# Row maxima of two attention units found during the projection ahead of them, and paced gathers and loads

## The chip, the cores and the metric

The kernel runs on one core of a Trainium2 chip. The metric is the time of one execution on the device in microseconds (us). The engines are TensorE (PE, matrix products and transposes), VectorE (DVE), ScalarE (ACT), GpSimd (POOL) and SyncE (SP, which only issues transfers here). They run side by side and wait for one another by semaphores.

## The reference

Two layers, cut to what is computed. `x` is 2 x 2048 tokens of 256 values.

```python
x  = L0_attn_x
xn = layernorm(x)
s  = linear_attention(xn, W_qkv, W_out)       # elu features, 16 heads
g  = silu(block(xn, ...))                     # 4 x 512 softmax heads of 16, then 8 experts:
                                              #   x + moe(layernorm(x + attn @ Wproj))
x  = x + s * g
xn = layernorm(x)
q, k, v = ((xn @ W).reshape(B, N, 16, 32).transpose(0, 2, 1, 3) for W in (Wq, Wk, Wv))
scores = where(causal, q @ k.T / sqrt(16), -inf)          # 2 x 16 heads, 2048 x 2048
s  = (softmax(scores) @ v) ... @ Wo
w  = simulate_quantize_int4(kernel)
g  = silu(xn @ w + bias + (xn @ a) @ b)
return x + s * g
```

## The kernel before

The program is a sequence of stages, each with one instruction stream for each engine, written out in the order in which that engine works: the first projection, an attention with heads of 16 values, a projection and gate, the routing, the experts (1171 to 1632 us of the trace), `combine_and_project` (1636 to 1899), `wide_attention` (1902.7 to 2947) and the output. The change touches the last four of them but the output.

*Marks.* In `combine_and_project` every engine has a list of names (`pe_names`, `act_names`, `dve_names`). `step(name, ...)` raises that engine's semaphore; `pe_s.wait(act, "s 4")` makes ACT wait until PE has done everything up to `s 4`. A name is a job and a number: `nT m` turns two tiles of the first attention's result (pair m, 16 of them), `s m` is the product of that pair with `w_out`; then for each block b of 512 tokens (8 of them) `qA`, `qB`, `kA`, `kB`, `vA`, `vB` are the halves of the three projections, `T b+1` turns the normalised block for the next round, `y b` is the feed-forward product. Jobs take PSUM banks in turn from two pools: `bank` (3 of them) for the products and `rot` (a single one) for the turnings. A job can take a bank only when the engine named beside the job before has emptied it.

*Combining stage* (the first part of it). PE alternates `nT` and `s`. ACT copies both out of PSUM (L2562, L2567). POOL gathers the experts' rows for 32 tiles, two indirect transfers each (L2549), into four places of two halves; the first eight wait for `nT n+1`. SP loads x (L2507) and the weights, each behind a mark of PE. DVE forms `mixed` (gates by gathered rows, L2640 and L2642), `x` (L2657, L2659), the moments, and `z`, the normalised block (L2678).

*Projection*. For each block ACT takes the upper half (`hi`, f16) of q and k out of the bank, DVE the rest (`lo`, L2685); so q and k are stored as two f16 parts each, `qhi`, `qlo`, `khi`, `klo` (L2532). Blocks 0 to 3 are batch 0, 4 to 7 batch 1. When block 4 comes to be stored, SP loads all that the attention's first group needs (six parts of q and k, four small rows, V; `load_group`) into the tiles `carried.q`, `carried.k` and `carried.v`.

*Second attention* (`wide_attention`). The 32 heads are 8 groups of four; each group has four units, unit u being the 512 queries from 512u on. A unit goes through these steps: score items `S` (PE at L1032, into one of three banks `at_s`), of which DVE takes the row maxima: at L966 where the causal mask is added (the last key block of a unit), at L972 where it is not; a sum of maxima and a shift `M`; the turning `T` of the shifts on PE (L1068), copied by DVE into a strip (L995) that SP writes into two more rows of q with four transfers (L862); then key tiles `ST` (PE, L1040 and the mask at L1044), whose result ACT turns into exponentials (L946), and products with V (L1094). The eviction of a unit is at L928. Which of these comes next on PE is set by a planner in `wide_schedule`, which simulates the engines with assumed costs and writes one list, `body`, that all engines follow. `T` of a unit can only come when all its maxima are known, and `ST` only when its strip has been written.

*Loads of the attention*. SP issues all seven loads of a group at one place: group 1 behind the second strip, group g+2 when group g has ended.

## Time and profile before

| | |
|---|---|
| three runs | 2997.93, 3001.39, 3002.08 us; median 3001.39 |
| the profiled execution | 3008.54 us, its span in the trace 3006.4 us |
| mean granted clock of PE | 0.969 |
| PE busy | 2831.9 us (94% of the span), 18017 matmuls |
| DVE busy | 2010.2 us (67%) |
| ACT busy | 1545.3 us (51%) |
| POOL busy | 990.0 us (33%) |
| DMA | 200.77 MB, mean 67 GB/s |
| chain that ended last, points of the span by engine | PE 29, DVE 4, ACT 1, issue 1, POOL 1 |

### The profile page before, as it was taken

The numbers are of one execution on the slowest core, as the hardware profiler recorded it, in microseconds if no ns is written. First come the engines' busy times: TensorE is split into PE (matmuls) and PEld (weight loads), VectorE is DVE, ScalarE is ACT, GpSimd is POOL, SyncE is SP. The second block draws the span as 40 slices with busy tenths as digits, with TensorE's granted clock in tenths as the row PEclk, the third lists the DMA queues.
The fourth block names the chain that finished last, engine by engine and source line by source line (L and its number), as shares of the span: only waits on it lengthen the run. The fifth ranks groups of instructions, "written<-read, shape, count | busy, mean of one in ns | idle before, by whom it ended". The sixth has DMA issues, their size and how long they took to land. (4 is left out here: it accounts for less than half of the span.)

```text
span 3006.4 us, 46248 instructions
## 1 busy us (share of the span) xinstructions
PE 2831.9 (94%) x18017; PEld 1317.3 (44%) x18017; DVE 2010.2 (67%) x4329; ACT 1545.3 (51%) x2581; POOL 990.0 (33%) x533
## 2 busy tenths in 40 slices
PE   7998999999999976999999899899999999999999
PEld 4664233333333344666676545323333333333327
DVE  7887899999999845000000565688787877878823
ACT  3452477676777755222222444345565665565571
POOL 1000000110101103111101330157777777777791
PEclk9997899999999987999999999889999999999999
DMA  4322122133202124232111466312020220202103
GB/s 130 97 77 76 37 51 39 43 62 66 50 24 62 24 68 130 63 86 75 63 48 34 148 193 185 79 32 61 8 64 12 68 64 8 64 12 68 67 12 119
DMA packets 141306, 200.77 MB, mean 67 GB/s; under 512 B 14320, under 2 KB 107904, under 8 KB 138000
## 3 DMA queue, kind: packets, MB, share of 16 engines
q1 hardware_dynamic: 130672, 173.21, 20.9%
q0 software_dynamic: 9056, 24.59, 3.9%
q8 instruction: 143, 2.34, 0.3%
q14 instruction: 75, 0.61, 0.1%
q10 hardware_dynamic: 1360, 0.01, 0.0%
HBM read 121.21 MB, written 76.02 MB: 66 GB/s over the span
## 5 line engine op out<-in xcount | busy, mean ns | idle before, releaser
L946 ACT ACTIVATE at_probs<-at_st 128x512 f32<-128x512 f32 (+3 forms) x1280 | 588.5, 542 | 442.1 <-PE at_st L1040 282.4
L909 POOL TENSOR_TENSOR at_probs<-at_probs 128x2048 f32<-128x2048 f32 (+3 forms) x205 | 725.9, 3546 | 214.7 <-ACT at_probs L946 135.4
L393 DVE TENSOR_REDUCE at_part<-at_s 128x1 f32<-128x512 f32 (+3 forms) x1280 | 690.0, 603 | 63.0 <-PE at_s L431 28.6
L368 ACT ACTIVATE at_probs<-at_st 128x1024 f32<-128x1024 f32 (+3 forms) x640 | 541.6, 895 | 275.4 <-PE at_st L450 141.0
L972 DVE TENSOR_REDUCE at_part<-at_s 128x1 f32<-128x512 f32 x768 | 498.5, 683 | 67.8 <-PE at_s L1032 63.9
L966 DVE CUSTOM_DVE_ANT_0 at_s<-at_s,at_later 128x384 f32<-128x384 f32 (+3 forms) x512 | 246.9, 498 | 103.8 <-PE at_s L1032 102.4
L510 PE MATMUL at_acc<-at_probs,at_v 128*32 128x512 f32 (+3 forms) x2560 | 305.5, 551 | 8.2 <-ACT at_otile L355 7.8
L2358 DVE TENSOR_TENSOR ex_ot<-ex_bank,lin_b 128x512 f32<-128x512 f32 x32 | 22.2, 692 | 426.3 <-PE ex_bank L2388 352.2
L2321 ACT ACTIVATE ex_hT<-ex_bank,ex_b 128x512 f32<-128x512 f32 x128 | 87.9, 687 | 334.7 <-PE ex_bank L2378 332.7
L2378 PE MATMUL ex_bank<-ex_xT,lin_w 128*128 128x512 f32 x512 | 225.5, 598 | 1.0 <-ACT ex_xT L2314 1.0
L2388 PE MATMUL ex_bank<-lin_w,ex_hT 128*128 128x256 f32 x1024 | 223.7, 379 | 0.8 <-ACT ex_hT L2321 0.8
L1032 PE MATMUL at_s<-all_k,all_q 96*128 96x512 f16 (+3 forms) x640 | 199.4, 366 | 15.1 <-DVE at_part L972 6.1
L2388 PEld LDWEIGHTS ex_bank<-lin_w,ex_hT 128*128 128x128 f32 x1024 | 193.9, 190 | 31.1 <-issue 3.8
L1040 PE MATMUL at_st<-all_q,all_k 98*128 98x512 f16 (+3 forms) x640 | 194.9, 362 | 6.6 <-ACT at_probs L946 3.8
L1032 PE MATMUL at_s<-at_kT,at_qT 96*128 96x512 f16 (+3 forms) x640 | 192.3, 356 | 8.3 <-DVE at_part L966 3.8
L431 PE MATMUL at_s<-lin_k_first,lin_q_first 48*128 48x512 f16 (+3 forms) x640 | 184.6, 374 | 14.9 <-DVE at_part L393 5.8
L1040 PE MATMUL at_st<-at_qT,at_kT 98*128 98x512 f16 (+3 forms) x640 | 185.1, 350 | 8.3 <-ACT at_probs L946 6.8
L431 PE MATMUL at_s<-at_kT,at_qT 48*128 48x512 f16 (+3 forms) x640 | 176.4, 361 | 6.9 <-DVE at_part L393 4.2
L1864 POOL DMA_DIRECT2D att_sums<-att x28 | 14.5, 523 | 487.7 <-DMA att<-at_otile 487.7
L2549 POOL DMA_INDIRECT p_rows<-exp_out,all_gather_at x64 | 62.1, 970 | 270.3 <-PE p_rot L2731 182.3
L2378 PEld LDWEIGHTS ex_bank<-ex_xT,lin_w 128*128 128x128 f32 x512 | 98.2, 192 | 118.2 <-issue 117.5
L1094 PE MATMUL at_acc<-at_probs,at_v 128*32 128x512 f32 (+3 forms) x1280 | 144.4, 536 | 4.0 <-ACT at_otile L928 3.8
(342 smaller groups left out, 3950.0 us busy)
## 6 DMA issues: line engine op xcount, KB each, us to landing
att<-at_otile SPq DMA_DIRECT2D x64, 256.0 KB, 2.1
lin_w<-in_W SPq DMA_DIRECT2D x16, 1024.0 KB, 7.5
at_v<-v SPq DMA_DIRECT2D x11, 1024.0 KB, 11.1
v<-pr_vt SPq DMA_DIRECT2D x32, 256.0 KB
exp_out<-ex_ot SPq DMA_DIRECT2D x32, 256.0 KB, 2.1
v<-p_vt SPq DMA_DIRECT2D x32, 256.0 KB, 3.7
p_xs<-in_x SPq DMA_DIRECT2D x8, 512.0 KB, 5.2
qhi<-p_parts SPq DMA_DIRECT2D x8, 512.0 KB
```

Source lines behind the costliest of these rows:

```text
L368: act.activation(probs[:, quad % RING, heads_down * p:heads_down * (p + 1), off:QB], st_ps[n % st_slots][:, :, off:QB], ACT.Exp, scale=EXP ...
L393: dve.tensor_reduce(part[:, w % 2, qt * HG + h, j:j + 1], s_ps[n % S_SLOTS][:, 0:width], AX.X, ALU.max).then_inc(item_free, 1)
L431: mm = pe.matmul(place[:, 0:width], QT[g % 2][rows, h // heads_down, q0:q0 + P], KT[g % 2][rows, h // heads_down, j * QB:j * QB + width], ...
L510: mm = pe.matmul(acc_ps[32 * h:32 * h + 32, off:QB], V[g % 2][:, kc, 32 * h:32 * h + 32], probs[:, quads % RING, h, off:QB], start=kc == 0 ...
L909: pool.tensor_tensor(total, total, probs[:, slots.slot[quad], :, off:QB], ALU.add).then_inc(add_done, 1)
L946: act.activation(probs[:, slots.slot[quad], h, off:QB], st_ps[n % ST_SLOTS][:, off:QB], ACT.Exp, scale=EXP_SCALE).then_inc(exp_done, 1)
L966: dve.tensor_tensor_reduce(out=s_ps[n % S_SLOTS][:, 0:width], in0=s_ps[n % S_SLOTS][:, 0:width], in1=later[:, QB - width:QB], scale=1.0, s ...
L972: dve.tensor_reduce(part[:, w % 2, qt * HG + h, j:j + 1], s_ps[n % S_SLOTS][:, 0:width], AX.X, ALU.max).then_inc(item_free, 1)
L1032: pe.matmul(place[:, 0:width], QT[g % 2][0:K, h, q0:q0 + P], KT[g % 2][0:K, h, j * QB:j * QB + width], start=True, stop=True).then_inc(ite ...
L1040: mm = pe.matmul(place[:, off:QB], KT[g % 2][0:K + 2, h, kc * P:(kc + 1) * P], QT[g % 2][0:K + 2, h, u * QB + off:(u + 1) * QB], start=Tru ...
L2378: mm = pe.matmul(d[:, :], w1[e % 2][:, n, f * P:(f + 1) * P], xT[:, n, cb * QB:(cb + 1) * QB], start=n == 0, stop=n == NF - 1)
L2388: mm = pe.matmul(d[:, t * D:(t + 1) * D], hT[cb][:, n, (2 * m + t) * P:(2 * m + t + 1) * P], w2[e % 2][:, n, :], start=n == 0, stop=n == N ...
```

## The change

Six things are done.

1. The row maxima of group 0's units 0 and 1 (`EARLY = 2`) leave `wide_attention`. They become 20 jobs `S 0` to `S 19` of the projection, each put behind one half of blocks 4 (`y` only), 5, 6 and 7, and each in the single `rot` bank. DVE takes the maxima (`max i`), and the two shifts. PE turns these in that bank (`row 0` behind `vB 5`, `row 1` behind `vB 7`), DVE copies the strips, SP writes them into `carried.q`. `S 0` waits for the six loads of q and k.
2. For that the loads of the first group are split: three parts behind the q stores of block 4, three behind its k stores, the small rows behind its v stores, V behind those of block 5.
3. The gathers of the combining stage wait for PE's marks one after the other, instead of the first eight only and the rest by half sets; SP's loads there come one pair earlier, `silu 0` and `sqrt 0` earlier on ACT, and DVE does the whole of block 0 before block 1's `mixed`.
4. In `wide_attention` the loads of the next group are eight pieces (V in halves), one issued at every fourth `ST`.
5. The planner's assumed delay after a group's last product goes from 12000 to 24000.
6. In the experts, the gathers for the second expert wait for marks of the first.

On PE, blocks 4 to 6 of the projection. L2770 and L2778 are the q, k and v halves, L2749 is `T`, L2788 is `y`; before, from `y 4` to `y 5`:

```order
L2788 MATMUL p_bank<-p_w_ffn,p_xT 128x256 x8
L2770 MATMUL p_bank<-p_xT,p_w 128x512 x16
L2778 MATMUL p_bank<-p_w,p_xT 128x512 x8
L2749 MATMUL p_rot<-all_identf,p_z 128x128 x8
L2788 MATMUL p_bank<-p_w_ffn,p_xT 128x256 x8
```

The same place now, from `y 4` to `kB 5` (L2958 is `y`, L2937 the q and k halves, L2898 an early score job):

```order
L2958 MATMUL p_bank<-p_w_ffn,p_xT 128x256 x8
L2898 MATMUL p_rot<-all_k,all_q 128x128 x4
L2937 MATMUL p_bank<-p_xT,p_w 128x512 x4
L2898 MATMUL p_rot<-all_k,all_q 128x256 x4
L2937 MATMUL p_bank<-p_xT,p_w 128x512 x4
L2898 MATMUL p_rot<-all_k,all_q 128x384 x2
L2937 MATMUL p_bank<-p_xT,p_w 128x512 x4
L2898 MATMUL p_rot<-all_k,all_q 128x384 x2
L2937 MATMUL p_bank<-p_xT,p_w 128x512 x4
L2898 MATMUL p_rot<-all_k,all_q 128x512 x2
```

What was one run of sixteen matmuls is four of four, with a score job in `rot` behind each.

On SP, around block 4, before (L744 are the group's loads of q and k, L2532 the stores):

```order
L744 DMA all_q<-qhi 32x4x2048
L744 DMA all_k<-klo 32x4x2048
L746 DMA all_k<-in_shift_rows 2x2048 x4
L748 DMA all_v<-v 128x2048
L2532 DMA qhi<-p_parts 128x4x512
L2532 DMA qlo<-p_parts 128x4x512
```

and now (L767 the loads, L2617 the stores of q and k, L2624 those of v):

```order
L2617 DMA qhi<-p_parts 128x4x512
L2617 DMA qlo<-p_parts 128x4x512
L767 DMA all_q<-qhi 32x4x2048
L767 DMA all_k<-khi 32x4x2048
L767 DMA all_q<-qlo 32x4x2048
L2617 DMA khi<-p_parts 128x4x512
L2617 DMA klo<-p_parts 128x4x512
L767 DMA all_k<-khi 32x4x2048
L767 DMA all_q<-qhi 32x4x2048
L767 DMA all_k<-klo 32x4x2048
L2624 DMA v<-p_vt 128x4x128 x4
```

All loads stood ahead of block 4's stores; they now stand three behind the q stores and three behind the k stores, in the same queue.

On PE, at the start of the second attention, before (L1032 `S`, L1068 `T`; the masked items of unit 0 first, by width):

```order
L1032 MATMUL at_s<-all_k,all_q 128x128 x4
L1032 MATMUL at_s<-all_k,all_q 128x256 x4
L1032 MATMUL at_s<-all_k,all_q 128x384 x4
L1032 MATMUL at_s<-all_k,all_q 128x512 x5
L1032 MATMUL at_s<-all_k,all_q 128x128
L1032 MATMUL at_s<-all_k,all_q 128x512
L1032 MATMUL at_s<-all_k,all_q 128x128
L1068 MATMUL at_s<-all_ident_f,at_shift 8x128 x4
```

and now (L1074 `S`, L1082 and L1086 `ST` and its mask):

```order
L1074 MATMUL at_s<-all_k,all_q 128x512 x2
L1074 MATMUL at_s<-all_k,all_q 128x128
L1082 MATMUL at_st<-all_q,all_k 128x512
L1086 MATMUL at_st<-all_mask_kq,all_ident 128x128
L1082 MATMUL at_st<-all_q,all_k 128x512
L1086 MATMUL at_st<-all_mask_kq,all_ident 128x128
```

Key tiles of unit 0 now come after three items (of unit 2) instead of twenty and a turning. By count, the items and key tiles that stand ahead of each `T` are: before, unit (0,0) 20 and 0, (0,1) 52 and 16, (0,2) 100 and 48, (0,3) 164 and 96, (1,2) 212 and 132; now (0,2) 52 and 48, (0,3) 116 and 96, (1,2) 164 and 160, (1,3) 244 and 224. From (2,1) on, 389 key tiles in, both lists are the same but for the 48 items that left.

The diff, cut to its core:

```diff
@@ -543,6 +543,28 @@
+EARLY = 2
+
+
+def early_jobs_of(u):
+    jobs = []
+    for qt in range(4):
+        for j in range(u + 1):
+            width = QB if j < u else (qt + 1) * P
+            together = 4 if width <= QB // 2 else 2
+            jobs += [(u, qt, h, together, j, width) for h in range(0, HG, together)]
+    return jobs
+
+
+EARLY_JOBS = [job for u in range(EARLY) for job in early_jobs_of(u)]
+EARLY_LAST = [max(i for i, job in enumerate(EARLY_JOBS) if job[0] == u) for u in range(EARLY)]
+EARLY_SLOTS = [(slot, b) for b, slots in ((4, "y"), (5, "qA qB kA kB vA y"), (6, "qA qB kA kB vA vB T y"), (7, "qA qB kA kB vA"))
+               for slot in slots.split()]
+EARLY_AT = {at: i for i, at in enumerate(EARLY_SLOTS)}
+EARLY_TURN = {("vB", 5): 0, ("vB", 7): 1}
+assert len(EARLY_SLOTS) == len(EARLY_JOBS)
+
+
 def wide_schedule():
@@ -638,7 +660,7 @@
                 if g >= 2:
-                    ready = max(ready, pv_end[last_of[g - 2]] + 12000)
+                    ready = max(ready, pv_end[last_of[g - 2]] + 24000)
...
@@ -731,33 +753,40 @@
+    def load_group(self, eng, C, qk, v, n):
         K = 32
...
+        if n < 6:
+            dst, src = (self.q, self.k)[n % 2], (qk[0][0], qk[1][0], qk[0][1], qk[1][0], qk[0][0], qk[1][1])[n]
+            eng.dma_start(dst[n // 2 * K:(n // 2 + 1) * K, :, :], src[0].rearrange("h d t -> d h t")).then_inc(self.qk_ld, 16)
+        elif n == 6:
+            for h in range(HG):
+                eng.dma_start(self.k[3 * K:3 * K + 2, h, :], C["shift_rows"][2 * h:2 * h + 2, h, :]
+                              ).then_inc(self.group_ld, 16)
+        else:
+            eng.dma_start(self.v[:, :, :], v[0, 0]).then_inc(self.group_ld, 16)
...
@@ -827,18 +856,24 @@
-        def load(eng, g):
-            eng.dma_start(V[k][:, :, :], v[g]).then_inc(v_ld[k], 16)
+            if n < 6:
+                r = n // 2
+                dst, src = (QT, KT)[n % 2], (q_hi, k_hi, q_lo, k_hi, q_hi, k_lo)[n]
+                eng.dma_start(dst[k][r * hd:(r + 1) * hd, :, :], src[g].rearrange("h d t -> d h t")).then_inc(qk_ld[k], 16)
+            else:
+                part = slice(NKC // 2 * (n - 6), NKC // 2 * (n - 5))
+                eng.dma_start(V[k][:, part, :], v[g][:, part, :]).then_inc(v_ld[k], 16)
+
+        LOADS, EVERY = 8, 4
...
                             sp.wait_ge(out_stored[k], issued[k])
-                        carried.load_finish(sp, W, out)
+                elif ev[0] == "ST":
+                    pairs += 1
+                    if pairs % EVERY == 0 and group:
+                        if loaded < (LOADS if group < GROUPS else Carried.FINISH_PARTS):
+                            sp.wait_ge(st_ready, pairs)
+                            if group < GROUPS:
+                                load(sp, group, loaded)
+                            else:
+                                carried.load_finish(sp, W, out, loaded)
+                            loaded += 1
+            assert group == GROUPS and loaded == Carried.FINISH_PARTS
             while ended:
...
@@ -2295,8 +2341,10 @@
-            for e, cb in ((0, 1), (1, 0), (1, 1)):
-                gather_tokens(pool, z_rows, rows_at, xin, rows_ld, e, cb)
+            gather_tokens(pool, z_rows, rows_at, xin, rows_ld, 0, 1)
+            for cb, f in ((0, half - 1), (1, NFF - 1)):
+                pe_s.wait(pool, f"h0{f} 0")
+                gather_tokens(pool, z_rows, rows_at, xin, rows_ld, 1, cb)
             for e in range(E - 2):
...
@@ -2413,6 +2461,7 @@
+    GROUP_AT = {(4, "q"): 3, (4, "k"): 3, (4, "v"): 1, (5, "v"): 1}
...
-    act_after = {9: ["silu 0"], 12: ["sqrt 0"], 15: ["silu 1"]}
+    act_after = {7: ["silu 0"], 10: ["sqrt 0"], 15: ["silu 1"]}
...
-    dve_names += ["mixed 0", "x 0", "moments 0", "mixed 1", "z 0", "x 1", "moments 1"]
+    dve_names += ["mixed 0", "x 0", "moments 0", "z 0", "mixed 1", "x 1", "moments 1"]
...
@@ -2506,14 +2591,14 @@
-            pe_s.wait(sp, "s 4")
+            pe_s.wait(sp, "s 3")
             load_x(0)
             for n, name in enumerate(("Wq", "Wk", "Wv")):
-                pe_s.wait(sp, f"s {2 * n + 6}")
+                pe_s.wait(sp, f"s {2 * n + 5}")
                 sp.dma_start(w[:, n], W[name].rearrange("(c p) n -> p c n", p=P)).then_inc(w_ld[0], 16)
             pe_s.wait(sp, "s 11")
             load_x(1)
...
@@ -2524,27 +2609,46 @@
                 for side, name in enumerate("qk"):
                     dve_s.wait(sp, f"lo {name}B {b}")
...
+                    for _ in range(GROUP_AT.get((b, name), 0)):
+                        carried.load_group(sp, C, qk_out, v_out, group)
+                        group += 1
                 act_s.wait(sp, f"vB {b}")
                 for g in range(4):
                     sp.dma_start(v_out[s, g, :, 4 * j:4 * j + 4, :], vt[:, :, g * P:(g + 1) * P]).then_inc(v_kept, 16)
+                for _ in range(GROUP_AT.get((b, "v"), 0)):
+                    carried.load_group(sp, C, qk_out, v_out, group)
+                    group += 1
+                for u in range(EARLY):
+                    if b == NB - EARLY + u:
+                        dve_s.wait(sp, f"strip {u}")
+                        for h in range(HG):
+                            sp.dma_start(carried.q[96:98, h, u * QB:(u + 1) * QB], strip[2 * h:2 * h + 2, u, :]
+                                         ).then_inc(carried.row_ld, 16)
             sp.wait_ge(part_out, 64 * NB)
             sp.wait_ge(v_kept, 64 * NB)
+            sp.wait_ge(carried.row_ld, 16 * HG * EARLY)
 
         @block.gpsimd
...
                 if b >= 2:
                     dve_s.wait(pool, f"mixed {b - 2}")
-                else:
-                    pe_s.wait(pool, f"nT {n + 1}")
+                if 0 < n < 12:
+                    pe_s.wait(pool, f"nT {n + n // 2}" if n < 11 else "T 0")
+                elif n:
+                    pe_s.wait(pool, f"{('qB', 'kB', 'vB', 'y')[t]} {b - 3}")
...
@@ -2632,6 +2736,41 @@
+            def maxima(i):
+                u, qt, h, together, j, width = EARLY_JOBS[i]
+                pe_s.wait(dve, f"S {i}")
+                tile, row = rot.tile(f"S {i}"), qt * HG + h
+                if i == 0:
+                    dve.wait_ge(later_ready, 1)
+                if j < u:
+                    last = dve.tensor_reduce(part[:, u, row:row + 2, j:j + 1], tile[:, :, 0:width], AX.X, ALU.max)
+                else:
+                    for y in range(together):
+                        place = early_place(tile, y, together, width)
+                        last = dve.tensor_tensor_reduce(out=place, in0=place, in1=later[:, QB - width:QB], scale=1.0,
+                                                        scalar=MASK, op0=ALU.add, op1=ALU.max,
+                                                        accum_out=part[:, u, row + y, j:j + 1])
+                step(f"max {i}", last)
+
...
+            def early(s, b):
+                if (s, b) in EARLY_AT:
+                    i = EARLY_AT[s, b]
+                    maxima(i)
+                    if i in EARLY_LAST:
+                        shifts(EARLY_LAST.index(i))
+                if (s, b) in EARLY_TURN:
+                    u = EARLY_TURN[s, b]
+                    pe_s.wait(dve, f"row {u}")
+                    step(f"strip {u}", dve.tensor_copy(strip[:, u, :],
+                                                       rot.tile(f"row {u}")[0:2 * HG, 0, 0:QB // 2].bitcast(F16)))
+
             def mixed_tile(b, t):
...
@@ -2705,13 +2844,19 @@
+                    early("qB", b)
                     lower(0, "q", "B", b)
+                early("kA", b)
                 lower(1, "k", "A", b)
                 if b + 2 < NB:
...
                     combine(b + 2)
                     statistics(b + 2)
+                early("kB", b)
                 lower(1, "k", "B", b)
+                for s in ("vA", "vB", "T"):
+                    early(s, b)
                 pe_s.wait(dve, f"y {b}")
                 if b:
                     act_s.wait(dve, f"g {b - 1}")
...
@@ -2740,6 +2886,27 @@
+
+            def early(s, b):
+                if (s, b) in EARLY_AT:
+                    i = EARLY_AT[s, b]
+                    u, qt, h, together, j, width = EARLY_JOBS[i]
+                    d = rot.take(pe, f"S {i}")
+                    if i == 0:
+                        pe.wait_ge(carried.qk_ld, Carried.QK_LOADS)
+                    for y in range(together):
+                        mm = pe.matmul(early_place(d, y, together, width),
+                                       carried.q[0:96, h + y, u * QB + qt * P:u * QB + (qt + 1) * P],
+                                       carried.k[0:96, h + y, j * QB:j * QB + width], start=True, stop=True)
+                    step(f"S {i}", mm)
+                if (s, b) in EARLY_TURN:
+                    u = EARLY_TURN[s, b]
+                    dve_s.wait(pe, f"shift {u}")
+                    d = rot.take(pe, f"row {u}")[0:2 * HG, 0, 0:QB // 2].bitcast(F16)
+                    for qt in range(4):
+                        mm = pe.transpose(d[:, qt * P:(qt + 1) * P], shift[:, u, qt * HG:(qt + 1) * HG, :]
+                                          .rearrange("p h two -> p (h two)"), C["ident_f16"][:, :])
+                    step(f"row {u}", mm)
 
             def turn(b):
...
```

## Rows read from the trace of the kernel before

**Rows 1.** The timeline of PE in the combining stage (start us, us, engine, instruction, idle before).

```profile
1655.86 0.60 PE L2731 MATMUL p_rot<-all_identf,all_mix 128*128 128x128 f32 x4
1658.02 0.60 PE L2731 MATMUL p_rot<-all_identf,all_mix 128*128 128x128 f32 x4
...
1678.85 0.60 PE L2731 MATMUL p_rot<-all_identf,all_mix 128*128 128x128 f32 x4
```

**Rows 2.** Windows there (PE, PEld, DVE, ACT, POOL busy; granted clock; DMA share; GB/s).

```profile
1660.00:1665.00 5.00, 0.77 (x5) 0.42 (x4) 0.00 (x0) 1.19 (x2) 3.78 (x5) 0.98 0.38 110
1665.00:1670.00 5.00, 3.65 (x11) 2.70 (x9) 0.00 (x0) 0.00 (x0) 3.78 (x5) 0.68 0.40 105
```

**Rows 3.** The timelines of ACT, SP and POOL there, one row each.

```profile
1673.81 0.60 ACT L2567 ACTIVATE all_mix<-p_bank 128x512 f32<-128x512 f32 x1 [9.28 <-remote]
...
1673.80 0.37 SPq L2513 DMA_DIRECT2D p_w<-in_Wk  x1
...
1669.81 0.95 POOL L2549 DMA_INDIRECT p_rows<-exp_out,all_gather_at  x1 [0.30 <-issue]
```

**Rows 4.** The timeline of PE in the projection: starts of blocks 5 and 6.

```profile
1824.05 10.46 PE L2770 MATMUL p_bank<-p_xT,p_w 128*128 128x512 f32 x24
1835.28 3.70 PE L2770 MATMUL p_bank<-p_xT,p_w 128*128 128x512 f32 x8 [0.76 <-DVE p_parts L2685]
...
1850.01 13.90 PE L2770 MATMUL p_bank<-p_xT,p_w 128*128 128x512 f32 x32
```

**Rows 5.** Windows of the second attention, from eviction to eviction.

```profile
1902.70:1942.00 39.30, 31.45 (x142) 10.95 (x143) 33.01 (x106) 8.25 (x18) 7.85 (x5) 0.69 0.04 6
1902.70:2083.10 180.40, 163.10 (x924) 53.84 (x924) 153.51 (x386) 79.75 (x168) 96.06 (x31) 0.86 0.13 30
2209.80:2334.60 124.80, 121.51 (x832) 40.88 (x832) 101.88 (x253) 74.78 (x166) 96.49 (x30) 1.00 0.18 43
```

**Rows 6.** The chain of waits: from the first strip to the first key tile.

```profile
1913.72 0.30 DVE at_strip L995
...
1915.93 1.59 DMA all_q<-at_strip
1917.57 0.61 PE at_st L1040
```

**Rows 7.** The chain of waits: three score matmuls of 512.

```profile
1947.00 0.65 PE at_s L1032 x3
```

**Rows 8.** The chain of waits: row maxima of 128 and of 512 columns.

```profile
1904.37 0.19 DVE at_s L966
...
1910.76 0.59 DVE at_s L966
...
2099.02 1.30 DVE at_part L972 x2
```

**Rows 9.** The timeline of DVE in blocks 5 and 6 of the projection.

```profile
1799.43 0.17 DVE L1195 RECIPROCAL p_rstd<-p_std 128x4 f32<-128x4 f32 x1
...
1805.37 0.48 DVE L2642 SCALAR_TENSOR_TENSOR p_fg<-p_rows,all_gate,p_fg 128x256 f32<-128x256 f32 x1
...
1811.56 1.22 DVE L2657 TENSOR_TENSOR p_fg<-p_fg,all_mix 128x1024 f32<-128x1024 f32 x1
...
1817.02 1.28 DVE L2685 SCALAR_TENSOR_TENSOR p_parts<-p_bank,all_score,p_parts 128x1024 f16<-128x1024 f32 x1
```

**Rows 10.** Windows around the loads of the first group.

```profile
1794.00:1802.00 8.00, 8.00 (x34) 5.43 (x33) 3.54 (x11) 4.24 (x4) 0.00 (x0) 1.00 0.97 297
1802.00:1818.00 16.00, 15.23 (x36) 6.52 (x35) 13.17 (x25) 7.49 (x8) 0.00 (x0) 1.00 1.04 202
```

**Rows 11.** The timeline of SP: block 4's q stores are issued.

```profile
1810.48 0.39 SPq L2532 DMA_DIRECT2D qhi<-p_parts  x1
```

**Rows 12.** The timeline of DVE: the strips of units (0,2) and (0,3).

```profile
1970.02 0.41 DVE L995 COPY at_strip<-at_s 8x512 f16<-8x512 f16 x1
...
2018.56 0.37 DVE L995 COPY at_strip<-at_s 8x512 f16<-8x512 f16 x1
```

More of the change, by code:

```diff
@@ L552, in wide_schedule @@
     ahead, late, count = [], None, {}
-    for unit in units:
+    for unit in units[EARLY:]:
         g, u = unit
@@ L578, in wide_schedule @@
     free, evictions = [0.0, 0.0], []
-    exp_end, pv_end, row_at, add_end, sum_end = [], [], {}, [], []
+    exp_end, pv_end, row_at, add_end, sum_end = [], [], {unit: 0.0 for unit in units[:EARLY]}, [], []
     slots = Slots(units)
@@ L841, in _ @@
             ended, issued = [], [0, 0]
+            pairs, group, loaded = 0, 1, 0
             def store(unit):
@@ L2427, in combine_and_project, with early_turns @@
             jobs.append((f"s {m - 2}", "act", f"s {m - 2}"))
+    turns = [(f"nT {m}", "act", f"nT {m}") for m in range(PAIRS)] + [("T 0", "act", "T 0")]
+    def early_turns(at):
+        if at in EARLY_AT:
+            turns.append((f"S {EARLY_AT[at]}", "dve", f"max {EARLY_AT[at]}"))
+            pe_names.append(turns[-1][0])
+        if at in EARLY_TURN:
+            turns.append((f"row {EARLY_TURN[at]}", "dve", f"strip {EARLY_TURN[at]}"))
+            pe_names.append(turns[-1][0])
     for b in range(NB):
@@ L2496, in combine_and_project @@
         marks = {"act": act_s, "dve": dve_s}
[L2497 to L2498 removed]
+        rot = Banked(c, "rot", [(n, (marks[e], d)) for n, e, d in turns], 1)
         banks = Banked(c, "bank", [(n, (marks[e], d)) for n, e, d in jobs], 3)
@@ L2772, in _ @@
                         step(f"{s}{half} {b}", mm)
+                        early(f"{s}{half}", b)
                 for half in "AB":
```

128 lines of the change are left out of this document (81 added, 47 removed).

## The prediction

> **What bounds the kernel now.** I read the page's shares first, then the windows by stage, then the chain of waits and the timelines at the three places that the change touches. The shares stand in the table above: TensorE (PE) is busy 94% of the span, and of the 36 points that the chain names it has 29. So time is won only where PE stands still, runs at its lower clock, or has less to do. Three places matter.
>
> *Combining stage* (1636 to 1691 us). A turn `nT` and an output projection `s` take 2.17 us together, the distance of the turns at 1655.86 and 1658.02. Then the rhythm breaks: from 1658.02 to the turn at 1678.85 PE does three such pairs in 20.83 us instead of 6.51. 14.3 us are lost [rows 1]. The granted clock reads 0.68 in part of it, so PE worked at the 1.2 GHz level for much of that time, after 5 us in which it was almost idle [rows 2]. ScalarE (ACT), which frees PE's banks here, waited 9.28 us for something that the profile calls only "remote", and SP issued the load of Wk, which waits for PE's mark `s 8`, at 1673.80 although PE had issued that work by 1660.4. PE's marks thus arrived late, while POOL issued gather after gather without a pause, the last at 1669.81 [rows 3].
>
> *Projection* (1691 to 1899 us). PE works at full clock. It has one wait of 0.76 us a block before block 6 and none in blocks 6 and 7 [rows 4]. Whatever is put in here, PE pays at once.
>
> *Start of the second attention.* Up to the eviction of unit (0,0), 39.3 us hold 142 matmuls at a clock of 0.69; up to the eviction of unit (0,3), 180.4 us hold 924. Later a group of four units takes 124.8 us for 832 [rows 5]. At that pace these 924 matmuls would take 138.6 us: 41.8 are lost. The chain shows why. VectorE (DVE) finds the row maxima, PE turns them, SP sends strips, and only 14.9 us after the stage's start does the first key tile run [rows 6].
>
> **Projection, term by term.** The 20 early jobs are 48 matmuls with 18,432 columns in all (5120 for unit 0, 8192 + 5120 for unit 1). Three score matmuls of 512 take 0.65 us [rows 7], so these take 7.8. For the joints between f32 and f16 work I put 0.03 us a job, 0.6, and for the two turns of the shifts 0.3 each. Work: 9.0 us.
>
> The waits come from the single turning bank, which each early job holds until DVE has its maxima. One masked maximum takes DVE 0.25 us for 128 columns (0.19 and the 0.06 that follows it) and 0.65 for 512, two plain ones of 512 take 1.30 [rows 8]. On PE a half block is 3.43 us (32 matmuls in 13.90 with the tail of the last) [rows 4]. Step by step:
> - In block 5 `S 2` comes 7.3 us after `S 0` (two halves and `S 1`). By then DVE has to do four maxima (1.0), z and `mixed 7` (1799.43 to 1805.85, 6.4 [rows 9]) and four maxima of 256 (1.5), and with the hand-over of 0.2 that is 9.1: wait 1.8. The old wait of 0.76 goes in return.
> - `S 5` waits for the maxima of `S 4`, which stand on DVE behind combine and statistics of block 7 (1811.56 to 1817.02, 5.5): 1.9.
> - `T 6` waits for the strip of unit 0: 0.6.
> - In block 6 `T 7` follows `S 12` directly and waits for its maxima, 1.4; `S 13` follows `T 7` and waits for ACT's copy of it, 1.2.
>
> That is 6.9 less 0.8: 6.1 us. The other jobs have a half of 3.43 us between them, more than the 2.6 us of one pair of maxima and one lower half on DVE.
>
> **The load before `S 0`.** `S 0` waits for six loads of 0.52 MB. SP issues three behind the q stores of block 4 and three behind its k stores, in one queue. In the trace these loads run at 202 GB/s with the DMA engines full (share 1.04), stores and what goes with them at 297 [rows 10]. From the q stores at 1810.5 [rows 11]: 1.05 MB of stores 3.5 us, 1.57 MB of loads 7.8, so 1821.8; then k stores 3.5 and k loads 7.8, so 1833.1. PE is ready at about 1824.3, for block 5 starts at 1824.05 now [rows 4]. Wait 8.5 us; DVE stands behind `S 0` too, so hardly any of it is made good. Bounds 0 (the loads are through) and 10. The Trainium skill, "DMA: Bandwidth & Descriptors", section Bandwidth, gives 341 GB/s for a 1 MB transfer; by that estimate the loads would end near 1827, the wait would be 2.3 us and the sum 6 us lower. The trace doesn't agree, with 202 GB/s for the same kind of load.
>
> Projection in all: 9.0 + 6.1 + 8.5 = 23.6 us more; bounds 14 and 27. At its end SP sends unit 1's four strips behind the last v stores. Four issues and a landing of 1.59 take 3.5 us [rows 6], of which I put 0.9 on the path, because ACT's last gate comes beside them; bounds 0 and 3.5.
>
> **Attention.** 48 score items and two turns leave it. Unit (0,2) can be keyed once DVE has its maxima: 48 items and 4 of the next unit, 36 plain ones at 0.65 and 16 masked ones at 0.45 on average, 30.6 us; with the start, the shifts and two units' sums 36 us after the stage's start. Now its strip is copied at 1970.02, 67.3 us after the start: gain 31. From there to unit (0,3)'s strip at 2018.56 the same items stand in both orders: 48.5 us again [rows 12]. After it part is given back. The new order has done every key tile of group 0 before unit (1,2) has its strip, and the same before (1,3). For 3.9 us each time (strip copy at 1913.72 to key tile at 1917.57 [rows 6]) PE has only score items, at DVE's pace. Two such holes: 8 us. From unit (2,1) on both orders are the same. I take 31 - 8 = 23 us; bounds 15 (two more holes) and 50 (the 42 lost, and 8 for the work that leaves).
>
> The attention's loads now go out one for every fourth key tile. Their first use lies some 65 key tiles behind the first load, and SP's strips stand behind at most one load more: 0, bounds -3 and +2.
>
> **Combining stage, priced.** Gathers of two row sets, now issued every 1.25 us (0.95 and the 0.30 before it) [rows 3], follow PE's turns and stop when PE stops. Loads come one pair earlier. If the unbroken run of gathers makes the marks late, the 14.3 us go; I keep 13, because `silu 0` still stands between ACT's turns, only earlier. Bounds -15 and +3: block 3's last gather now waits for `y 0`, its rows land some 4.1 us later (two issues of 1.25 and a landing of 1.59), and DVE comes to them after y, z and six half tiles, 6.6 us (1.22, and 5.4 like 1799.43 to the tile before 1805.37 [rows 9]). If that cover goes, DVE, ACT and `kB` wait. In the experts the second expert's gathers wait for marks of the first one's hidden layer; the eight experts take 461 us, 58 each, so the rows are wanted half an expert or more later, and I count 0.
>
> **Sum.** 23.6 + 0.9 - 23 - 13 = -11.5 us on the profiled execution's 3008.5: 2997.0. The median of the runs shown is 7.1 lower: 2990.
>
> **Rivals.**
> - *Both covers hold (chance 0.22).* The loads are through before `S 0`, and the attention gives nothing back. For: PE comes into the attention at full clock, and only the 4096-byte part of the loads is slow. Against: the full queue at 1802 to 1818, and the order's two holes. 23.6 - 8.5 + 0.9 - 31 - 13 = -28: 2973.
> - *The late marks stay (0.27).* Gathers aren't their cause, or they appear under the profiler alone. For: the DMA engines were 0.40 busy there. Against: they end 3 us after the last gather. 23.6 + 0.9 - 23 = +1.5: 3003.
> - *Bank and load decide, the slower side (0.18).* PE waits for the k loads at `S 0` with DVE behind it, each later job gets the bank late (27 in all), and the holes leave 15 of the start's gain, while half of the combining gain comes: 27 + 0.9 - 15 - 6.5 = +6.4, 3008. It decides from a wait before `S 0` of over 6 us together with a gain at unit (2,1) under 18.
> - The forecast has 0.33.
>
> Likeliest 2990; range 2967 to 3010, the likeliest case's own 2982 to 2999. Less than 0.2% (6 us) can't be told from no change. Faster: all of the first rival, four fifths of the forecast, a tenth of the second, 0.52. Slower: two thirds of the third and a fifth of the second, 0.18. Same: the rest, 0.30.
>
> **What would show it.** Combining: the three pairs in 6.5 us at a clock near 1.0. Before `S 0`: a PE wait of 8 us on a load. Blocks 5 and 6: waits of 1 to 2 us on the turning bank. Attention: first key tile within 2 us, unit (0,2)'s strip 36 us and (0,3)'s 85 us after the start, then 124.8 us a group. I am wrong if the hole stands, if `S 0` doesn't wait, or if the gain at (0,3)'s strip is far from 31 us.

## The result, and the profile after

The changed kernel takes 3007.53 us (median of 20 executions), the kernel before 3001.26 (20, the same chip); ratio 1.0027, interval 1.002 to 1.0034. So it is slower by 6.3 us, where 11.5 less and 2990 were forecast. The profiled execution of the changed kernel took 3011.69, its span is 3010.0.

The two traces, cut at the first turning of the combining stage, at the first matmul of block 0, at the end of `y 7` and at the first score of the second attention (each read from PE's timeline):

| stage, us | before | changed | difference | forecast |
|---|---|---|---|---|
| all ahead of the combining stage | 1636.2 | 1643.7 | +7.5 | 0 |
| combining | 54.6 | 40.5 | -14.1 | -13 |
| projection, blocks 0 to 7 | 208.3 | 241.4 | +33.1 | +23.6 |
| from `y 7` to the first score | 3.9 | 4.5 | +0.6 | +0.9 |
| second attention to its last eviction | 1043.8 | 1020.4 | -23.4 | -23 |
| the rest | 59.6 | 59.6 | 0 | 0 |

The first line shows no effect of the change: in the 18 further profiles below this stretch takes 1635.2 to 1644.3 us, for kernels with and without the change alike. Its last part, from the experts' first matmul on, is where point 6 of the change lies, and it takes 463.8 to 465.4 us in all 20 profiles, so the scatter lies in stages that no edit touches, and point 6 is worth nothing that can be measured. Point 5 was not tried alone. The four lines below the first, in which the change can act, sum to -3.8. So this pair of profiles doesn't hold the result. One thing is odd about the profile of before: its execution, 3008.54 us, is longer than each of the 20 timed ones (2993.6 to 3004.0), and the record doesn't say on which chip it was taken. Something that it shows may be missing from those 20.

*Combining.* Windows of the changed kernel over the stretch that [rows 2] show, and POOL's timeline:

```profile
1660.00:1665.00 5.00, 5.00 (x31) 4.44 (x29) 0.78 (x2) 2.82 (x6) 2.58 (x4) 1.00 0.69 210
```
```profile
1651.95 0.96 POOL L2653 DMA_INDIRECT p_rows<-exp_out,all_gather_at  x1 [2.24 <-PE p_rot L2877]
...
1658.44 0.94 POOL L2653 DMA_INDIRECT p_rows<-exp_out,all_gather_at  x1 [1.79 <-PE p_rot L2877]
```

PE is busy throughout at 1.00, and POOL, which had issued sixteen transfers one behind the other before, now pauses for some 2 us after every four (two sets). The stretch in which PE stands still, called the hole from here on, is gone.

*Projection.* The timeline of PE, blocks 4 to 7:

```profile
1831.79 0.58 PE L2898 MATMUL p_rot<-all_k,all_q 96*128 96x128 f16 x4 [11.88 <-DMA all_k<-klo]
1832.16 5.67 PE L2937 MATMUL p_bank<-p_xT,p_w 128*128 128x512 f32 x8
...
1838.11 3.60 PE L2937 MATMUL p_bank<-p_xT,p_w 128*128 128x512 f32 x8
...
1855.00 0.60 PE L2898 MATMUL p_rot<-all_k,all_q 96*128 96x512 f16 x2 [1.89 <-DVE p_part L2750]
...
1859.95 1.06 PE L2916 MATMUL p_rot<-all_identf,p_z 128*128 128x128 f32 x8 [0.60 <-DVE p_strip L2771]
...
1889.38 1.06 PE L2916 MATMUL p_rot<-all_identf,p_z 128*128 128x128 f32 x8 [1.41 <-DVE p_part L2746]
1891.56 1.04 PE L2898 MATMUL p_rot<-all_k,all_q 96*128 96x512 f16 x2 [1.11 <-ACT p_xT L2686]
1892.39 6.23 PE L2958 MATMUL p_bank<-p_w_ffn,p_xT 128*128 128x256 f32 x16
```

The waits in the bank are where they were forecast and nearly as long (`S 5` 1.89 against 1.9, `T 6` 0.60 against 0.6, `T 7` 1.41 against 1.4, `S 13` 1.11 against 1.2). Two things are not as forecast. `S 0` waited 11.88 us for the last load of k, not 8.5, and after that idle stretch the next eight matmuls took 5.67 instead of 3.60. And `y 6` took 6.23 instead of 3.62 behind the two waits at `T 7` and `S 13`. The windows show the clock there: 0.63 and 0.56 granted in the last two, between the levels of 1.2 and 2.4 GHz.

```profile
1819.00:1832.00 13.00, 1.12 (x8) 0.70 (x7) 1.23 (x1) 1.06 (x1) 1.89 (x2) 0.64 1.06 278
1832.00:1837.70 5.70, 5.70 (x13) 2.46 (x11) 5.01 (x21) 0.00 (x0) 0.00 (x0) 0.63 0.75 202
1892.40:1898.40 6.00, 6.00 (x17) 4.78 (x16) 1.23 (x1) 0.00 (x0) 0.00 (x0) 0.56 0.13 40
```

*Second attention.* The windows that answer to [rows 5], counted from the first score at 1930.0, and the strips of units (0,2) and (0,3), which answer to [rows 12]:

```profile
1930.00:2072.80 142.80, 133.93 (x847) 43.90 (x847) 109.67 (x258) 76.39 (x166) 96.11 (x31) 0.96 0.15 36
...
2212.50:2337.90 125.40, 122.50 (x843) 41.59 (x841) 104.81 (x256) 74.42 (x165) 96.82 (x31) 1.00 0.17 43
```
```profile
1967.80 0.41 DVE L1037 COPY at_strip<-at_s 8x512 f16<-8x512 f16 x1
...
2013.33 0.37 DVE L1037 COPY at_strip<-at_s 8x512 f16<-8x512 f16 x1
```

The first key tile runs 0.9 us after the first score. Unit (0,2)'s strip comes 37.8 us after it (36 were forecast), unit (0,3)'s 83.3 (85 were forecast), 32 less than before. After two groups 24.3 us of that are left, at the end 23.4. The forecast had 31 and 23.

### The profile page after: what moved, and what is told of

Same layout as the page of the kernel before. It is cut to its first block and busy times, and to the rows that moved or that the text cites. A ratio compares the mean times of both kernels' runs of the same rounds, so it can differ in the third digit from the quotient of the medians.

```text
span 3010.0 us, 46280 instructions
## 1 busy us (share of the span) xinstructions
PE 2832.8 (94%) x18017; PEld 1319.8 (44%) x18017; DVE 2014.0 (67%) x4321; ACT 1543.5 (51%) x2581; POOL 988.3 (33%) x535
## 5 line engine op out<-in xcount | busy, mean ns | idle before, releaser
L1014 DVE TENSOR_REDUCE at_part<-at_s 128x1 f32<-128x512 f32 x752 | 487.5, 683 | 67.9 <-PE at_s L1074 63.6
L1008 DVE CUSTOM_DVE_ANT_0 at_s<-at_s,at_later 128x128 f32<-128x128 f32 (+1 forms) x480 | 231.8, 498 | 106.6 <-PE at_s L1074 105.6
L1074 PE MATMUL at_s<-at_kT,at_qT 96*128 96x512 f16 (+3 forms) x640 | 190.6, 354 | 7.7 <-DVE at_part L1014 3.0
L1082 PE MATMUL at_st<-all_q,all_k 98*128 98x512 f16 (+3 forms) x640 | 190.6, 355 | 7.6 <-ACT at_probs L989 4.6
L1082 PE MATMUL at_st<-at_qT,at_kT 98*128 98x512 f16 (+3 forms) x640 | 187.6, 352 | 10.4 <-ACT at_probs L989 7.8
L1074 PE MATMUL at_s<-all_k,all_q 96*128 96x512 f16 (+3 forms) x592 | 178.7, 357 | 10.7 <-PEq L43 4.5
L1140 PE MATMUL at_acc<-at_probs,all_v 128*32 128x512 f32 (+3 forms) x1280 | 143.5, 538 | 2.8 <-ACT at_otile L971 2.8
```

Of the source, the lines that this page charges most:

```text
L1014: dve.tensor_reduce(part[:, w % 2, qt * HG + h, j:j + 1], s_ps[n % S_SLOTS][:, 0:width], AX.X, ALU.max).then_inc(item_free, 1)
L1074: pe.matmul(place[:, 0:width], QT[g % 2][0:K, h, q0:q0 + P], KT[g % 2][0:K, h, j * QB:j * QB + width], start=True, stop=True).then_inc(ite ...
L1082: mm = pe.matmul(place[:, off:QB], KT[g % 2][0:K + 2, h, kc * P:(kc + 1) * P], QT[g % 2][0:K + 2, h, u * QB + off:(u + 1) * QB], start=Tru ...
L1140: mm = pe.matmul(acc_ps[32 * h:32 * h + 32, off:QB], V[g % 2][:, kc, 32 * h:32 * h + 32], probs[:, slots.slot[quads], h, off:QB], start=kc ...
```

## The experiments

Each row gives the median, that of the kernel before in the same call, and the ratio of the two with its interval. Runs without an interval had one execution. The letter says which ran together, and each letter is a chip of its own; the chip of the result above is not on record. a0 and a1 are the changed kernel again, b0 and b1 the kernel before; `_again` and `_third` repeat the run of the same number, and e6 repeats e4, whatever its name says.

| run | us | before | ratio |
|---|---|---|---|
| A e1_combining_only | 3000.29 | 3012.89 | 0.9956 (0.9944 to 0.9969) |
| A e2_without_combining | 3018.29 | 3012.89 | 1.0016 (1.0002 to 1.0030) |
| A e3_loads_first | 2995.05 | 3012.89 | 0.9932 (0.9913 to 0.9950) |
| A e4_attention_loads_at_once | 3006.17 | 3012.89 | 0.9977 (0.9964 to 0.9990) |
| B b0_before_again | 3010.92 | 3014.07 | one execution |
| B a0_after_again | 3005.65 | 3014.07 | 0.9982 (0.9970 to 0.9995) |
| B e5_gathers_only | 2997.76 | 3014.07 | 0.9951 (0.9938 to 0.9963) |
| B e6_loads_first_at_once | 3009.66 | 3014.07 | one execution |
| C a1_after_third | 3007.76 | 3002.49 | 1.0023 (1.0014 to 1.0033) |
| C e3_again | 2997.21 | 3002.49 | 0.9987 (0.9976 to 0.9998) |
| C e7_gathers_only_early | 2998.15 | 3002.49 | 0.9990 (0.9978 to 1.0002) |
| C e8_slot_moved | 2999.97 | 3002.49 | 0.9991 (0.9982 to 1.0000) |
| D b1_before_third | 3009.93 | 3014.84 | one execution |
| D e5_again | 3002.54 | 3014.84 | 0.9954 (0.9937 to 0.9971) |
| D e1_again | 3001.83 | 3014.84 | 0.9954 (0.9937 to 0.9970) |
| D e2_again | 3018.39 | 3014.84 | 1.0011 (0.9999 to 1.0024) |
| E e2_third | 3022.72 | 3014.26 | 1.0019 (1.0005 to 1.0032) |
| E e5_third | 3000.74 | 3014.26 | 0.9957 (0.9945 to 0.9969) |

**e1 and e2, the combining part alone and left out.** e1 is the kernel before with all edits of point 3 of the change and no other; e2 is the changed kernel without them. Of SP's loads in that point four come one pair earlier; the second of x stays, and that of the bias comes one pair later.

> The kernel before with the combining stage's part of the change alone (gathers paced by PE's marks, loads one pair earlier, silu 0 and sqrt 0 earlier, DVE's block 0 whole before block 1). Theory A, the hole of 14.3 us is in every execution of the kernel before and pacing removes it: 14 us faster, ratio about 0.995. Rival B, the hole is in some executions only, or mostly in profiled ones: within 4 us, ratio 0.999 to 1.001. Rival C, pacing costs something that one profile does not show: slower than before.

> The changed kernel with the combining stage's part undone, all else kept. Theory A: 14 us slower than the changed kernel, so 20 to 22 slower than before, ratio 1.007. Rival B: about as the changed kernel, ratio 1.002 to 1.004. Its profile also shows whether the hole comes back in a second program.

e1 is 12.6 us faster than before, e2 5.4 slower. The combining stage takes 41.7 us in e1's profile and 54.9 in e2's. That is theory A for e1. For e2 the forecast of 20 to 22 us slower failed: it is 12.1 us above e4 below, which stands for the changed kernel in this call, but only 5.4 above the kernel before. For here the kernel before takes 3012.89, and it had taken 3001.26.

e2's profile shows one thing more. PE's timeline in e2_again, and POOL's in the changed kernel, of which six transfers fall between block 4's q stores (1806.25) and `S 0` (1831.79):

```profile
1835.95 0.58 PE L2896 MATMUL p_rot<-all_k,all_q 96*128 96x128 f16 x4 [9.32 <-DMA all_k<-klo]
```
```profile
1809.46 1.08 POOL L2653 DMA_INDIRECT p_rows<-exp_out,all_gather_at  x1 [5.85 <-PE p_bank L2937]
...
1821.91 0.94 POOL L2653 DMA_INDIRECT p_rows<-exp_out,all_gather_at  x1 [0.30 <-issue]
```

In e2's three profiles no gather falls there, and `S 0` waits 9.2 to 9.4 us; in the five profiles of the changed kernel and of e4 it waits 11.8 to 12.2. So point 3 costs some 2.5 us of that wait, and the six gathers are what it puts there; that they do it is argued, for e2 undoes the whole point.

**e3, all loads first.** The eight parts of `load_group` go back ahead of block 4's stores:

```diff
+                    for group in range(8):
+                        carried.load_group(sp, C, qk_out, v_out, group)
-                    for _ in range(GROUP_AT.get((b, name), 0)):
...
```

> The changed kernel with all loads of the first group ahead of block 4's stores again, as in the kernel before. Theory: the wait of 11.88 us before S 0 and the low clock behind it go, some 14 us, of which the later stores give a little back: 12 us faster than the changed kernel, ratio to before 0.998 to 0.999. Rival: block 4's q and k stores, now behind 4.2 MB of loads, hold ACT at block 5 and PE's banks with it, and the time stays: ratio 1.002 to 1.003.

It is the fastest kernel of the call, 0.9932, and 11.1 us below e4; the ratio of 0.998 to 0.999 was expected for a kernel before that takes 3001. PE's timeline:

```profile
1814.18 0.39 PE L2892 MATMUL p_rot<-all_k,all_q 96*128 96x128 f16 x4
...
1824.57 0.82 PE L2892 MATMUL p_rot<-all_k,all_q 96*128 96x384 f16 x2 [2.64 <-DVE p_part L2744]
1825.18 4.79 PE L2931 MATMUL p_bank<-p_xT,p_w 128*128 128x512 f32 x8
```

`S 0` doesn't wait. `S 2` does now, as the forecast had it for loads that are through (2.64 us, forecast 1.8), and the eight matmuls behind it took 4.79 us instead of 3.60. The rival, stores that hold ACT at block 5, shows no wait here.

**e4, e6: the attention's loads at one place.** The same kernel twice:

```diff
-                    if pairs % EVERY == 0 and group:
-                        if loaded < (LOADS if group < GROUPS else Carried.FINISH_PARTS):
-                            sp.wait_ge(st_ready, pairs)
+                    if group:
+                        while loaded < (LOADS if group < GROUPS else Carried.FINISH_PARTS):
```

> The changed kernel with the second attention's loads issued at one place again (group 1 at the stage's start, group g+2 when group g has ended) instead of one for every fourth key tile. Theory: pacing is worth nothing, 0 within 2 us of the changed kernel, ratio 1.0027. Rival 1: the planner's list has its first use late enough only for early loads, so pacing costs and this is 3 us or more faster. Rival 2: strips now stand behind eight loads, and this is 3 us or more slower, most of it at units (0,2) and (0,3).

> The changed kernel with the second attention's loads at one place, a second look beside the changed kernel itself. Theory: within 2 us of the changed kernel's profile, stage by stage. Rival: over 3 us apart.

From the first score to the last eviction e4 takes 1021.4 us, e6 1019.6, the changed kernel 1020.4 to 1020.7 in three profiles. Pacing these loads is worth nothing, as forecast. e6's profile is 7.8 us longer than that of a0 beside it; 7.9 of these lie ahead of the combining stage (1644.3 against 1636.4), so the rival's bound was met by scatter only.

**The kernel before and the changed kernel again.**

> The kernel before, unchanged, for a second profile. The comparison of the kernel before across chips (3001.3 on the first, 3012.9 on the second) is 11.6 us. Theory: that difference is the hole of the combining stage, which is in the profile here as well, 12 to 15 us long. Rival: the combining stage is like the first profile's or shorter and the rest of the program is slower.

> The changed kernel on the chip on which its parts are compared. Theory: its time hardly depends on the chip, because it has no hole, so 3006 to 3008 here too, ratio 0.998 where the kernel before takes 3013; early maxima, their load and the combining part add up as 0.9956 x 1.0016 / 1 = 0.997. Rival: ratio 1.002 to 1.003 as first measured, and then the parts do not add up.

> The changed kernel, beside e3_again, e7 and e8 on one chip. Theory: its own time stays at 3005 to 3008 us; what differs between chips is the kernel before (3001 or 3013), by the length of its hole. So the ratio is 0.998 or 1.002, by the time of the kernel before here. Rival: the changed kernel's time moves with the chip and the ratio is steady.

On B the change is 0.18% faster, on C 0.23% slower. Its own time is 3005.65, 3007.76 and 3007.53; the kernel before takes 3001.26 and 3002.49 in two calls and 3012.89 to 3014.84 on the four other chips. The sign of the result hangs on the kernel before. In each of its profiles, and in those of e2, the hole is there, at other places and in several pieces. In b0's timeline of PE:

```profile
1653.49 1.03 PE L2731 MATMUL p_rot<-all_identf,all_mix 128*128 128x128 f32 x4 [1.96 <-ACT all_v L2562]
...
1667.37 1.11 PE L2731 MATMUL p_rot<-all_identf,all_mix 128*128 128x128 f32 x4 [3.31 <-ACT all_v L2562]
...
1676.59 1.11 PE L2731 MATMUL p_rot<-all_identf,all_mix 128*128 128x128 f32 x4 [5.22 <-ACT all_v L2562]
```

Combining takes 54.6, 56.9 and 53.5 us in the three profiles of before, and 54.9, 55.3, 57.0 in those of e2. In the fourteen profiles with paced gathers it takes 40.4 to 41.8.

**e5, the gathers alone.** Of point 3 only this is kept:

```diff
-                else:
-                    pe_s.wait(pool, f"nT {n + 1}")
+                if 0 < n < 12:
+                    pe_s.wait(pool, f"nT {n + n // 2}" if n < 11 else "T 0")
+                elif n:
+                    pe_s.wait(pool, f"{('qB', 'kB', 'vB', 'y')[t]} {b - 3}")
```

> The kernel before with the pacing of the gathers alone; SP's marks, silu 0, sqrt 0 and DVE's order as before. Theory: the unbroken run of gathers makes the hole, so this gives most of the combining part's 13 us: ratio 0.996 to 0.997, and no hole in its profile. Rival: ACT's or SP's earlier place or DVE's order removes it, and this gives nothing: ratio 0.999 to 1.001, with the hole.

0.9951 with no hole, its combining stage 40.5 us. So the gathers issued without a pause make the hole. Why PE's marks arrive late beside them no run shows. The earlier marks for SP and ACT and DVE's order add nothing that can be measured (e1 0.9956, overlapping). Some of the gain is given back: the projection takes 211.2 to 212.5 us in e5's three profiles, 208.3 to 209.5 in those of before.

**e7 and e8, ways to do better.** e7 is e3 with the gathers alone; e8 moves the slots of the early jobs:

```diff
-EARLY_SLOTS = [(slot, b) for b, slots in ((4, "y"), (5, "qA qB kA kB vA y"), (6, "qA qB kA kB vA vB T y"), (7, "qA qB kA kB vA"))
+EARLY_SLOTS = [(slot, b) for b, slots in ((4, "T y"), (5, "qA qB kA kB vA y"), (6, "qA qB kA kB vA vB y"), (7, "qA qB kA kB vA"))
```

> All loads of the first group ahead of block 4's stores, on one chip with the changed kernel. Theory, from the profiles: the wait before S 0 (11.9 and 12.2 us) and 2.4 us of low clock behind it go, the wait of S 2 comes in with 2.6 and 1.4 of low clock: 10.3 us faster than the changed kernel. Rival: 15 us, as the two ratios to the kernel before on two chips have it (0.9932 against 0.9982).

> As e3_again, with only the gathers of the combining part kept (SP's marks, silu 0, sqrt 0 and DVE's order as in the kernel before). Theory: the gathers alone remove the hole, the rest of that part is worth nothing: within 2 us of e3_again. Rival: 3 us faster, as e5_gathers_only (0.9951) against e1_combining_only (0.9956) hints.

> As e7, with the early jobs one place earlier: S 0 behind the turning T 5 of block 4, and none behind the turning T 7 of block 6, so that block 6 has one wait less. Theory: the waits of 1.41 and 1.12 us at T 7 and S 13 and the low clock of y 6 (6.24 us instead of 3.62) go, a wait of 1.1 us for ACT's copy of T 5 comes in: 3 to 4 us faster than e7. Rival: the loads of q and k are not through at S 0's new place, or DVE's maxima pile up in block 5 instead: no difference or slower.

e3 is 10.55 us below the changed kernel on the same chip; 10.3 were expected from the profiles. e7 is within 1 us of e3. In e8's timeline the low clock of `y 6` is gone and one wait with it, but `T 7`'s stays:

```profile
1812.79 0.40 PE L2892 MATMUL p_rot<-all_k,all_q 96*128 96x128 f16 x4 [1.16 <-ACT p_xT L2680]
...
1826.89 0.50 PE L2892 MATMUL p_rot<-all_k,all_q 96*128 96x384 f16 x2 [2.56 <-DVE p_part L2744]
...
1875.11 1.06 PE L2910 MATMUL p_rot<-all_identf,p_z 128*128 128x128 f32 x8 [1.41 <-DVE p_part L2740]
1876.01 3.62 PE L2952 MATMUL p_bank<-p_w_ffn,p_xT 128*128 128x256 f32 x16
```

Its projection is 3.7 us shorter than e7's (227.4 against 231.1), as expected; its attention is 2.3 longer and its combining stage 1.2 longer, and the timed runs show no gain. The expectation of 3 to 4 us in all failed.

**Which chip, which kernel.** The remaining runs ask whether kernels with the hole move from chip to chip and those without stay.

> The kernel before once more, for its combining stage. If it takes about 3001 here: theory, the hole is absent or under 4 us in its profile, and its stage from the first turn to block 0 takes some 43 us instead of 54.6. Rival: the hole is there all the same, and another stage is 11 us shorter. If it takes about 3013: the hole is there with 14 us, as on the other such chips.

> Pacing of the gathers alone on the kernel before. Theory: its own time is 2998 whatever the chip, as the changed kernel's is 3006 to 3008; so 0.995 where the kernel before takes 3013 and 0.999 where it takes 3001. Rival: 0.995 everywhere.

> The combining stage's whole part alone. Theory: 3000 us whatever the chip, 2 us over e5_again, because the rest of that part moves nothing off the path.

> The changed kernel without the combining part, which has the same hole as the kernel before: 5 us over the kernel before on the first chip (1.0016). Theory: it moves with the kernel before, so 1.002 here as well; where the kernel before takes 3001 it takes 3006, not above the changed kernel's 3007. Rival: 3018 on every chip.

> The changed kernel with the combining part undone, once more, for a chip on which the kernel before takes 3001 to 3003. Theory (the difference between chips is the hole): there it takes 3006 to 3008, 11 us less than its 3018 on the other chips. Rival (the chip's difference lies elsewhere): 3018 there too. On a chip where the kernel before takes 3013 it only repeats 3018.

> The pacing of the gathers alone, beside e2_third. Theory: 2998 to 3002 on every chip, so within 3 us of the kernel before on a chip where that takes 3001 to 3003. Rival: 12 to 16 us below the kernel before there too.

Both calls met chips on which the kernel before takes 3014 to 3015. There the sorts of kernel lie apart as on A and B: with the hole 3010 to 3023, without it 2995 to 3003 (3006 with the changed kernel's loads). e5's own time isn't steady: 2997.76, 3002.54 and 3000.74, where 2998 was expected. What a kernel with the hole, other than the one before, takes on a chip of the other sort was not measured, and neither were e1 and e5. All that is shown of that sort is this: the kernels timed there without the hole (the changed one, e3) are within 2.2 us of their times elsewhere, and the kernel before is 10 to 14 us below. The four profiles of C don't have a shorter time ahead of the combining stage (1637.4 to 1641.8 us), in code that the kernel before shares up to the experts; that speaks for the hole. But that it is shorter there is argued, not shown: the kernel before was never profiled on C, and no profile of it has a combining stage under 53 us.

## Why the prediction was wrong

Two steps failed: the term of -13 for the combining stage, which was read from one execution and then applied to the median, and the term of +8.5 for the load before `S 0`, which left out traffic that the change itself moves there. Most of the other mechanisms were right. The measured 3007.53 lies inside the wide range (2967 to 3010) and outside the likeliest case's own (2982 to 2999).

- *The hole was counted from one execution, and then again in the step to the median.* The text took 13 us off the profiled execution's 3008.5 and then 7.1 more, "lower" than the profile, to reach the median. If the timed executions are 7 us shorter because their hole is, that 7.1 may not be taken off twice. The cause named (the run of gathers without a pause) was right, as e5 shows alone. Its worth is 12 to 16 us where the kernel before takes 3013 to 3015; on B, such a chip, the changed kernel is 8.4 us faster, so there the forecast had the sign right. Where the kernel before takes 3001 to 3002, an estimate is all there is: the lines of the table other than the first two sum to +10.3, the medians differ by +6.3 and +5.3, so the combining stage gave some 4 to 5 us instead of 13. Why it gave less there stays open.
- *The rivals.* The first (0.22) fell with the wait before `S 0` and with the 7.9 us that the attention gave back. The one that the marks stay late had 0.27 and 3003; "under the profiler alone" is refuted by e1 and e5, whose timed runs gain. The slower side had 0.18 and 3008, and the measured 3007.53 is next to it by luck: it asked for a gain under 18 us at unit (2,1), which was 24.3, and for jobs that get the bank late, which they didn't.
- *The load before `S 0` was mis-sized, and its aftermath left out.* The term was 8.5 us with 10 as its upper bound; the wait measured 11.88 (12.21 in a0). (By the text's own times, 1824.3 and 1833.1, the term should have been 8.8.) From the q stores (1806.25 in the changed kernel) PE came to `S 0` after 13.7 us, as forecast, but the loads were through after 25.5, not 22.6. In e2, where no gathers run beside the loads, they were through after 22.9 to 23.1: the sum was right for the stores and loads that it counted, and lacked what point 3 adds, six gathers, worth 2.5 of the 3.4 us. `S 2`'s 1.8 us didn't come, because PE came to it 9.8 us after `S 0` and not 7.3, behind the slow half. DVE was held up as forecast (idle for 11.2 us before `S 0`'s maxima) and was ready just in time. The clock that fell in the idle stretch cost 2.1 us on the next half (5.67 against 3.60); no term had it, though [rows 2] had shown the same thing. e3, which takes the wait away, is 10.55 us faster. The estimate by the Trainium skill's 341 GB/s ("DMA: Bandwidth & Descriptors", Bandwidth) erred further: it had the wait at 2.3 us.
- *Block 6.* The waits were right, the low clock of `y 6` behind them was not foreseen: 2.6 us. It isn't there each time: in the eleven profiles with these two waits `y 6` takes 6.21 to 6.29 us in six, 4.62 to 4.83 in four and 3.62 in one (a0).
- *Blocks 0 to 4* took 2.5 us more, with paced gathers (e5's profile has 2.1 of it without any early job). It had been bounded by +3 and counted as 0. Of it 1.7 is `y 0`: 5.41 us in all fourteen profiles with paced gathers, 3.72 in five of the six others, behind waits of about the same length. The excess of these items, 3.4 + 2.1 + 2.6 + 2.5 less 1.8, is 8.8 us; the projection and the 0.6 behind it measured 9.2 more than forecast (33.7 against 24.5).
- *Attention.* 24.3 and 23.4 us against 23. The size was right, the reason for what is given back in part. The two gaps between strip and key tile are there, with score items in them: from the strip's copy of unit (1,2) to its first key tile PE idles 0.9 us of 4.7, at unit (1,3) 1.9 of 3.9, 2.7 together and not 7.8. Another 3.3 us of 9.3 are of a kind that had no term (last section). Of the 32.2 us gained at unit (0,3)'s strip 7.9 were given back, so some 2 us are traced to no wait. The windows:

```profile
2067.03:2071.76 4.73, 3.86 (x19) 1.13 (x19) 4.34 (x19) 0.00 (x0) 2.26 (x2) 1.00 0.02 5
2123.37:2127.30 3.93, 2.07 (x12) 0.56 (x13) 3.75 (x12) 0.00 (x0) 1.27 (x1) 1.00 0.01 2
2143.70:2153.00 9.30, 6.04 (x44) 1.46 (x36) 9.27 (x5) 2.56 (x5) 8.09 (x2) 1.00 0.00 0
```

- *The early maxima* do earn with e3's loads: e3 is 5.2 us below e1 on A, and below the kernel before on both sorts of chip (by 17.8 us on A, 5.3 on C). Of the kernels tried it is the one to keep. On a chip like C it was not compared with the paced gathers alone.

## What to carry to other kernels

Before a stall seen in one profile is priced, look for it in a second profile, and ask whether the timed executions have it: where the profiled one is longer than all of them, the stall may be the difference. Work put ahead of its data costs the idle time and then the lower clock behind it (11.9 and 2.1 us here). So place a load where its bytes are through before the consumer comes, at the measured rate and with the other traffic counted, above all the traffic that the same change moves there. Transfers issued in an unbroken run went with late marks of another engine here: pace them by their use, and look at where they land then.

## What the hardware showed unexpectedly

A tiny operation on DVE that starts while POOL works can last until POOL's ends. In the changed kernel the shift of one unit (16 values a partition, two operands in SBUF, 0.2 us elsewhere) took 3.65 us, and the one behind it 4.45, while POOL added 128x2048 tiles. DVE's and POOL's timelines:

```profile
2045.95 4.23 DVE L1024 SCALAR_TENSOR_TENSOR at_shift<-at_rowmax,at_nothing 128x16 f16<-128x16 f32 x1
2050.21 0.18 DVE L1028 SCALAR_TENSOR_TENSOR at_shift<-at_rowmax,at_shift 128x16 f16<-128x16 f32 x1
...
2143.70 3.65 DVE L1024 SCALAR_TENSOR_TENSOR at_shift<-at_rowmax,at_nothing 128x16 f16<-128x16 f32 x1
2147.38 4.45 DVE L1028 SCALAR_TENSOR_TENSOR at_shift<-at_rowmax,at_shift 128x16 f16<-128x16 f32 x1
```
```profile
2045.60 4.54 POOL L952 TENSOR_TENSOR at_probs<-at_probs 128x2048 f32<-128x2048 f32 x1 [1.53 <-ACT at_probs L989]
```

The shift that starts at 2045.95, inside this POOL operation, ends at 2050.18, POOL's at 2050.14. In the second attention all 18 shifts over 1 us in this trace, and all 16 in that of before, end 33 to 46 ns after an operation of POOL that had started ahead of them. So DVE's shift waits for the rest of POOL's operation. The Trainium skill, "SBUF — State Buffer", section "SBUF: two separate sides", has a lock of this sort between the two engines, held for a whole instruction by whichever starts first, for DVE operations with two SBUF inputs against POOL operations that read SBUF. The trace agrees for POOL ahead of DVE. Between unit (1,1)'s maxima and its strip (copied at 2153.75) two such waits follow each other here, 8.1 us in all, and PE then waits 2.69 us:

```profile
2152.48 0.39 PE L1074 MATMUL at_s<-all_k,all_q 96*128 96x512 f16 x1 [2.69 <-DVE at_part L1014]
```
